# Four layers of attention and experts on one core: norms of layers 0 and 1 a slot earlier, a copy moved to ScalarE, a down product placed later, routed rows and turns dealt earlier

## What is computed

```python
x = x + _L0_xattn_ref(_layernorm(x), ctx, ...)   # cosine of projected rows and projected context
x = x + _L0_ffn_ref(_layernorm(x), ...)          # 8 gated experts of 336, a learned number of them per row
x = x + _L1_xattn_ref(_layernorm(x), ctx, ...)   # softmax attention, one head of 128
x = x + _L1_ffn_ref(_layernorm(x), ...)          # the best 2 of 8 experts of 512
x = x + _L2_xattn_ref(_layernorm(x), ctx, ctx, ...)   # 16 heads of 8
x = x + _L2_ffn_ref(_layernorm(x), ...)          # 2 of 8 gated experts, and a shared one
x = x + _L3_xattn_ref(_layernorm(x), ctx, ...)   # 16 heads of 8
x = x + _L3_ffn_ref(_layernorm(x), ...)          # 2 of 8 experts of 256
```

## Time and profile before

| | us |
|---|---|
| three runs | 2001.98, 2015.2, 2015.51 |
| median | 2015.2 |
| profiled execution | 2013.27 |
| its span (first to last instruction) | 2011.2 |
| TensorE busy in it | 1768.9 (88%) |
| VectorE busy | 1304.1 (65%) |
| ScalarE busy | 920.3 (46%) |
| GpSimd busy | 780.1 (39%) |

### The profile page before, as it was taken

How to read it: one execution, slowest core, us unless ns; L and a number is a source line. 1 busy time by engine, 2 the same in 40 slices (tenths; PEclk the granted TensorE clock), 3 DMA queues, 4 the chain that set the end, 5 groups by cost and what they waited for, 6 DMA issues and landing times. The chain is left out here.

```text
span 2011.2 us, 35857 instructions
## 1 busy us (share of the span) xinstructions
PE 1768.9 (88%) x10982; PEld 1372.5 (68%) x10982; DVE 1304.1 (65%) x3574; ACT 920.3 (46%) x3205; POOL 780.1 (39%) x803
## 2 busy tenths in 40 slices
PE   3899999999999998889898999899998998887874
PEld 1577677776777788766575887678777775564663
DVE  1567776777867643256676777678767686675643
ACT  1222222222222222287765566556565567776621
POOL 1445556565655621323242222322214224343444
PEclk9899999999989999899898999889999999997977
DMA  5605122520601088842015661276333535552766
GB/s 157 224 5 171 51 74 68 190 109 8 146 20 59 31 310 261 298 146 85 27 27 188 199 201 47 63 256 219 99 145 102 164 113 147 143 164 67 198 181 200
DMA packets 171307, 269.70 MB, mean 134 GB/s; under 512 B 24364, under 2 KB 103662, under 8 KB 170862
## 3 DMA queue, kind: packets, MB, share of 16 engines
q1 hardware_dynamic: 148894, 237.69, 37.2%
q0 software_dynamic: 12288, 25.19, 4.1%
q10 hardware_dynamic: 9936, 4.53, 0.8%
HBM read 202.44 MB, written 82.91 MB: 142 GB/s over the span
## 5 line engine op out<-in xcount | busy, mean ns | idle before, releaser
L1901 POOL DMA_INDIRECT list<-xn,pos x192 | 191.3, 997 | 323.1 <-DVE pos L1595 192.3
L1971 POOL TENSOR_TENSOR hid<-tg,uc 128x512 f32<-128x512 f32 x168 | 217.9, 1297 | 230.3 <-DVE tg L1684 229.2
L1255 ACT ACTIVATE probT<-B 128x512 f32<-128x512 f32 x256 | 158.6, 620 | 212.9 <-PE B L880 212.4
L1303 ACT ACTIVATE tg<-up 128x512 f32<-128x512 f32 x168 | 100.3, 597 | 299.1 <-PE up L994 286.4
L1003 PEld LDWEIGHTS Y<-wd,hid 128*128 128x128 f32 x1344 | 180.2, 196 | 72.9 <-issue 45.1
L1249 ACT ACTIVATE prob<-up,nmax 128x128 f32<-128x128 f32 x588 | 209.8, 392 | 2.9 <-DVE nmax L1446 2.9
L1681 DVE TENSOR_TENSOR uc<-up,ytmp 128x512 f32<-128x512 f32 x168 | 114.9, 684 | 143.2 <-PE up L994 125.2
L994 PE MATMUL up<-x2T,wg 128*128 128x512 f32 x336 | 200.8, 680 | 2.7 <-DVE tg L1684 2.7
L1788 DVE COPY xsT<-Y 128x128 f32<-128x128 f32 x262 | 75.1, 287 | 188.7 <-PE Y L1036 188.4
L1003 PE MATMUL Y<-wd,hid 128*128 128x128 f32 x1344 | 181.2, 279 | 5.7 <-DVE x L1689 5.6
L994 PE MATMUL up<-x2T,wu 128*128 128x512 f32 x336 | 180.1, 619 | 0.0
(11 more groups left out here) (243 smaller groups left out, 3960.6 us busy)
## 6 DMA issues: line engine op xcount, KB each, us to landing
w_tile<-wt SPq DMA_DIRECT2D x46, 768.0 KB, 4.7
list<-w_tile SPq DMA_DIRECT2D x21, 1536.0 KB, 14.3
w_tile<-wt SPq DMA_DIRECT2D x45, 512.0 KB, 5.3
w_tile<-wt SPq DMA_DIRECT2D x55, 321.0 KB, 3.5
wg<-list SPq DMA_DIRECT2D x262, 64.0 KB
wd<-wt SPq DMA_DIRECT2D x20, 768.0 KB
list<-wu SPq DMA_DIRECT2D x193, 64.0 KB
wd<-wt SPq DMA_DIRECT2D x16, 512.0 KB
```

What stands on the lines that cost most here:

```text
L1255: act.activation(probT[:, (2 * r + i) % 4, :, :], B4[:, :, :], ACT.Copy).then_inc(probT_done.sem, 1)
L1901: pool.indirect_dma_start(out=list_to(K, g)[:, :], in_=xn2[:, t, :], in_offset=None, out_offset=bass.IndirectOffsetOnAxis(ap=pos[:, g, s, ...
L1971: pool.tensor_tensor(hid[:, n % HRING, :], tg[:, n % 2, :], uc[:, n % 2, :], ALU.mult)\
```

## The change

Seven edits, none of which alters a value:

- VectorE normalizes layer 0's first norm at step 1 and layer 1's first at step 5.
- The copy of layer 1's transposed probabilities goes from VectorE's step 13 to ScalarE's step 13.
- In the slot in which a group's down products open, TensorE makes the down product after the small work instead of before it.
- SyncE's first row and weight loads wait for the last up product, and the weights of ring 7 for the last down product.
- Round 1's twenty early turns are dealt 3, 3, 4, 3, 2, 2, 1, 1, 1 to slots -9 to -1, before 2, 2, 3, 1, 3, 3, 2, 2, 2.

```diff
--- before.py
+++ after.py
@@ -97,6 +97,7 @@
 B1_AT, B2_AT = 512, 514
 WRING = 9
 WFRONT = 5
+RINGS_DOWN = WFRONT + 2
 
 
 
@@ -120,7 +121,7 @@
 
 
 
-DEALT = {0: [1] * 20 + [4, 5, 5, 4, 4], 1: [2, 2, 3, 1, 3, 3, 2, 2, 2] + [1] * 22, ALONE: [2, 2, 2, 2, 3, 3, 4]}
+DEALT = {0: [1] * 20 + [4, 5, 5, 4, 4], 1: [3, 3, 4, 3, 2, 2, 1, 1, 1] + [1] * 22, ALONE: [2, 2, 2, 2, 3, 3, 4]}
 DEALT_FROM = {0: OVER - 1, 1: -9, ALONE: 132}
 SLOTS = range(-10, PAIRS * len(CHAIN) + 2 * PAIRS)
 
@@ -641,7 +642,7 @@
                         sp.dma_start(w_shared[:, k * HIDDEN[2]:(k + 1) * HIDDEN[2]].rearrange("p (c r) -> p c r", r=P),
                                      d[name][:, CHUNKS[2] - 4:CHUNKS[2], :]).then_inc(shared_loaded, 16)
                 if g == GROUPS:
-                    sp.wait_ge(y_ready.sem, y_ready.at(0, GROUPS - 1, 1))
+                    sp.wait_ge(u_ready.sem, u_ready.at(0, GROUPS - 1, TRIP))
                     for done in zeroed:
                         sp.wait_ge(done, 16 * 7)
                     for *_, turns in in_trip(g):
@@ -695,6 +696,8 @@
                 e = row_of[n] >> (LIST.bit_length() - 1)
                 if r == 0:
                     sp.wait_ge(relaid, 16 * 20)
+                if r == RINGS_DOWN:
+                    sp.wait_ge(y_ready.sem, y_ready.at(0, GROUPS - 1, 1))
                 if r >= WRING:
                     m = max(k for k in range(n) if ROUTED_NO[k] == r - WRING)
                     sp.wait_ge(tile_y_read if TILES[m][0] == 3 else tile_y, m + 1)
@@ -1009,8 +1012,8 @@
                 for s, chunk, groups0, group1, s1, turns in in_trip(g):
                     if chunk is not None and chunk >= 2:
                         up_product(chunk)
-                    down, _ = due(g, s)
-                    if down is not None:
+                    down, complete = due(g, s)
+                    if down is not None and complete is None:
                         down_product(down)
                     tile_turns(turns)
                     for group0, s0 in groups0:
@@ -1022,6 +1025,8 @@
                         up_product(1)
                     if group1 is not None:
                         layer1(group1, s1)
+                    if down is not None and complete is not None:
+                        down_product(down)
 
             def transpose_rows(n):
                 r = ROUTED_NO[n]
@@ -1225,6 +1230,10 @@
                                          accum_out=sums[:, 0, t:t + 1])
                 ins.then_inc(exp_done.sem, 1)
 
+            def evacuate_probs1(g):
+                act.wait_ge(probT_psum.sem, probT_psum.at(1, g, 1))
+                act.activation(probT[:, 2, :, :], D4[:, :, :], ACT.Copy).then_inc(probT_done.sem, 1)
+
             def read_queries(K, g):
                 act.wait_ge(proj[K > 0].sem, proj[K > 0].at(K, g, 1))
                 act.activation(qT[:, g % 2, :], X[:, :], ACT.Identity, bias=bqs[:, K - 1:K], scale=float(HD) ** -0.5)\
@@ -1290,6 +1299,8 @@
                     read_values1(g)
                 if s == 12:
                     exponentials1(g)
+                if s == 13:
+                    evacuate_probs1(g)
                 if s == 19:
                     evacuate_norm(1, g, LN2)
                 if s == 22:
@@ -1437,10 +1448,6 @@
                 dve.wait_ge(score.sem, score.at(1, g, 1))
                 dve.tensor_reduce(nmax[:, 0, :], D4, AX.X, ALU.max, negate=True).then_inc(nmax_done.sem, 1)
 
-            def evacuate_probs1(g):
-                dve.wait_ge(probT_psum.sem, probT_psum.at(1, g, 1))
-                dve.tensor_copy(probT[:, 2, :, :], D4[:, :, :]).then_inc(probT_done.sem, 1)
-
             def score_max(K, g, r, i):
                 dve.wait_ge(score.sem, score.at(K, g, 2 * r + i + 1))
                 dve.tensor_reduce(nmax[:, (2 * r + i) % 4, :], scores_in(K, g, 2 * r + i), AX.X, ALU.max, negate=True)\
@@ -1619,7 +1626,7 @@
                     if g == 1:
                         dve.wait_ge(rest_loaded, REST)
                     norm_moments(0, g, LN1)
-                if s == 2:
+                if s == 1:
                     normalize(0, g, LN1)
                 if s == 6:
                     clamp_norms(g)
@@ -1649,12 +1656,10 @@
             def layer1(g, s):
                 if s == 4:
                     norm_moments(1, g, LN1)
-                if s == 6:
+                if s == 5:
                     normalize(1, g, LN1)
                 if s == 11:
                     score_max1(g)
-                if s == 13:
-                    evacuate_probs1(g)
                 if s == 14:
                     divide_rows1(g)
                 if s == 15:
```

## The result

| | before | after |
|---|---|---|
| runs beside each other, median (range) | 2013.72 (2001.98 to 2015.51) | 1955.14 (1953.05 to 1957.68) |
| ratio, 95% interval | | 0.9715 [0.969, 0.974] |
| profiled execution, its span | 2013.27, 2011.2 | 1957.68, 1955.9 |
| mean granted clock over the span | 0.942 | 0.951 |

A second profile of the changed kernel (experiment 1) shows the same.

A forecast was written before the change was run, and what follows sets the result against it. TensorE's instruction order was taken to set the pace in the trips, with DMA at 0.97 between 800 and 820 us. Terms 9.6 + 7.6 + 4.3 + 5.4 + 2.2 + 8.2 = 37.3 us off 2013.3 gave 1976.0 us, range 1958 to 2001.

The forecast's parts named there:

- Rival C: Trips: fewer stretches at the lower clock, so ended waits give more than their length; 12 us more, 1964; chance 0.08.
- Layer 0's norm: Trips, slot 1: VectorE normalizes sooner, so TensorE's 9.6 us wait in 6 places goes; -9.6, lower end -7.
- Probabilities: Trips: ScalarE copies layer 1's transposed probabilities some 1.8 us earlier, so TensorE's wait in 6 places goes whole; -7.6.
- Down product: Trips, 6 places: placed behind small products, its wait for VectorE's add goes, except 1.3 us in trip 7; -4.3.
- Layer 1's norm: Trips, slot 5: VectorE normalizes sooner, so TensorE's wait in 7 places goes; -5.4, lower end -3.
- Late next: Check of VectorE's work behind layer 1's moved norm: the next slot's two expert products still fit by 0.2 us.
- Rows sooner: Start of round 0: loads leave at least 2.3 us earlier, so the second row's transpose comes sooner; -2.2.
- More turns: Ahead of layer 2: four more turns before the combine, TensorE's 8.27 us stop becomes 2.0; -8.2, bounds 0 and -9.
- The same 1157 us: From the first score to the end: order unchanged, so the same 1157 us follow.
- Rival A: Early turns: loads hold the moved turns back, so the last two terms are nothing; 1986.4; chance 0.13.
- B: Trips: VectorE takes TensorE's place as the limit, half of 26.9 us comes back as waits; 1989.4; chance 0.17.
- D: Trips: thin products straight behind the up product bring more lower-clock stretches, 42 us lost; 2018; chance 0.04.

The follow-up runs named there:

- experiment 1: The changed kernel run and profiled again with no edit: 1956.69 us, ratio 0.9714.
- experiment 4: Kernel before with layer 0's first norm at step 1 alone: 2002.96 us; together with the moved opening down product: 1980.78 us.
- experiment 2: Opening down product behind the small products, alone on the kernel before: 1999.29 us; that edit taken out of the changed kernel: 1973.94 us.
- experiment 5: Kernel before with only the copy of layer 1's probabilities moved to ScalarE: 2005.73 us, ratio 0.9954.
- experiment 6: Changed kernel with layer 1's first norm back at step 6: 1964.16 us, ratio 0.9747.
- experiment 7: Changed kernel with round 1's early turns dealt as before: 1970.49 us, ratio 0.9784.
- experiment 3: Changed kernel with TensorE also awaiting VectorE's residual add ahead of the thin products, down product still behind them: 1973.21 us, ratio 0.9787.

## Why the prediction missed

The waits were right and the sum too small. The step that failed is the clock's term of the sum. The prediction took 2.9 us of clock, at the combine alone, and put it at nothing in the trips, where each wait was priced at its length. Rival C saw the possibility, but gave it a chance of 0.08 and 12 us on top of the forecast. It came, and larger: in the two profiles the lower level fell by 31.9 us in the trips and by 10.2 behind round 1's first row, worth some 16 and 5 us by the estimate of half. The mean clock of each run bears this out without the profile. Span times (1 - clock) is 122.5 us on average over 19 runs of before and 98.2 over 8 of after; beside the runs of before on the chip of experiment 1 it fell from 128.4. That is 24 us less, or 30 by the second comparison; what is left of the span fell by 34 or 26, where the forecast without its clock share is 34.4.

Edit by edit the times say the same. Apart from the others, the norm of layer 0, the down product and the probabilities gave 11.6, 14.3 and 8.8 us (experiments 4, 2 and 5); taken out of the changed kernel, layer 1's norm and the deal cost 7.5 and 13.8 (6 and 7). The sum is 56, the whole change 55 to 59. Each is above its forecast, the down product and the deal by most.

By its steps:

- *Layer 0's norm*, -9.6: right as a wait (10.0 us of idle less in experiment 4). Its share of the clock was missing.
- *Probabilities*, -7.6: right (7.9 less).
- *Down product*, -4.3: right as a wait (4.1 less, 1.5 of mask stay where I had 1.3). This is the term most mis-sized, 14.3 by the times: 0.7 us ahead of thin work costs several times that, 16.5 us for 5.6 in experiment 3.
- *Layer 1's norm*, -5.4: it fitted, with 1.5 us to spare, at 1.70 us for the norm. "Late next" was wrong: not the expert products but layer 0's residual add and second norm, 1.5 us.
- *Rows sooner*, -2.2: the second row came 2.4 us sooner, as worked out, but round 0 as a whole is only 0.8 shorter.
- *More turns*, -8.2: 10.3 in this profile, 6.4 in the second one; the wait is 2.76 instead of 2.0. The second one has 6.8 us at the lower clock there, half of it behind the row that came late.
- *The same 1157 us*: 1157.1 and 1157.6; 1153.5 in the second profile.

Rival A falls in the main: the second gather held VectorE by 0.82 us, and in the first profile no moved turn waited for its rows. In the second one did, for 2.31 us, which the prediction had named as a sign of being wrong. B falls: the waits for VectorE's products are 3.1. D falls: the thin run stands right behind the up product, and the lower level shrank. E is excluded by the waits. For C I cited the page "TensorE: Matmul & The Clock Gate", HAM oscillation, in the Trainium skill, that each fall of the clock between bursts is paid anew. These runs agree: in experiment 3 a stretch of 10.2 us stands at each of four passages. The page's example is a longer wait, for a DMA; here 0.72 us was enough where thin work follows.

Of the signs that the prediction named, "a trip is some 4 us shorter" showed the miss: from first cosine product to first cosine product they were 85.8 and 84.7 us apart (394.4, 480.2, 564.9 in the windows of before), and are 78.0 and 77.5 after: 7 to 8 us, too much for the waits alone. And the first score came at 798.3, not near 817.

What stays open: why three passages of the changed kernel still fall to the lower level, the same ones in both profiles, and why the stretch behind the first score takes 1151 to 1161 us in the profiles with an unchanged order, with 141 to 173 us at the lower level. No version ran faster than the changed kernel.

## What to carry to other kernels

Price a wait of TensorE by what stands behind it. Ahead of products of 128x128 and more, the waits for the probabilities were worth about their length; ahead of small matmuls, read the granted clock of the microseconds after the wait, and add half of the stretch at the lower level to it. Judge single edits by the times, not by the lower level in one profile: there, taking away either of two waits won 0 to 7 us of lower level and both together 34, while the times apart (11.6 and 14.3) all but add up to the 30.7 together. And a "busy" window says nothing of speed: count its matmuls or read its clock.

## What the hardware showed that I had not expected

A standstill of 0.72 us was enough for 10.2 us at 1.2 GHz behind it when thin products followed (experiment 3); the waits of up to 1.3 us for the probabilities, in front of products of 128x128, left the clock where it was (experiments 4 and 5).
